# Blocks of the turned node pairs copied from the X tile on the chip instead of loaded from DRAM, in a one-core graph layer

## The chip, the cores and the metric

The kernel runs on one core of a Trainium2 chip. The metric is the device time of one execution in microseconds (us), as the median over runs. The profile is of one further execution, whose span (first to last instruction) and device time are given below.

## What is computed

A graph layer over N = 50000 nodes with 512 features, in float32. Cut to what matters:

```python
msg  = x[src]                                    # 62500 edges, one of them a loop at every node
agg  = segment_sum(msg, dst, n);  deg = segment_sum(ones, dst, n)
mean = agg / maximum(deg, 1)[:, None]
h    = mean @ W_l + b + x @ W_r
out  = layernorm(x + h * sigmoid(h))             # over the 512 features
```

Only 12500 edges are not loops. The kernel therefore computes `x @ (W_l + W_r) + b` for all nodes, and a correction row for each of the few nodes that have other edges.

## The kernel before, in words

There are five in-order queues: SP (SyncE, which issues nearly all plain transfers), POOL (gathers by index and the small rstd work), PE (TensorE), ACT (ScalarE) and DVE (VectorE). An instruction waits on semaphores at the head of its queue, and all that stands behind it on that queue waits too. Every queue's order is written out by hand, step by step over t.

The nodes lie in 391 tiles of 128 rows. Three stages follow each other. In the **early stage** (to about 180 us) the products of the first 44 tiles are made and put into DRAM, while DVE works out index lists. In the **edge stage** (to about 503 us) 98 tiles of edges give the correction rows. In the **node stage** the remaining 347 tiles are worked off as NP = 174 pairs of tiles, and one of the 44 "light" tiles is finished in every fourth pair. The change touches the node stage and the last steps of the edge stage on SP.

A pair t goes through these steps, with the function and line of each:

- SP loads its 256 rows into slot t mod 4 of the tile `X` (`load_x`, L321). It first waits until `residual` of pair t-4 is done (`u_made`, L319), as that was the last reader of the slot.
- PE needs the pair with features on the partitions. For an even pair PE turns it itself: 8 transposes of `X` into PSUM (`transpose_x`, L634). An odd pair is turned "by blocks" (`by_blocks`, L206; 86 pairs, t = 1, 3, ..., 171): SP loads the rows once more from DRAM into `x_raw`, with blocks of 32 rows placed so that DVE's transpose of 32 x 32 blocks (`turn_blocks`, L1093, from `x_raw` into `x_blocks`) gives a usable order. For these pairs PE uses weights with permuted rows (`wb_hi`, `wb_lo`).
- ACT rounds the turned pair into `x_hi` (`round_x`, L791 for blocks, L795 otherwise), DVE makes the rest `x_lo` (`split_x`, L1081 and L1084).
- PE multiplies: 24 matmuls of 128x512 a pair (`three`, L530) onto a PSUM bank that ACT has seeded with the gathered correction rows (`seed`, L817).
- ACT applies silu (L829), DVE adds `X` (`residual`, L1110, which releases the slot of `X`), DVE takes moments (L1118, L1121), POOL makes rstd, DVE `shift` (L1128), ACT normalises into `O` (L805), SP stores `O` (`store_out`, L339).

What sets the order around the change:

- SP's step t (`move`, L374) is: load the blocks of pair t+3 if t+3 is odd; `load_x(t+3)`; `store_out(t-3)`; a store or two loads for the light tile. There is one buffer `x_raw`. `load_blocks(p)` waits until pair p-2 has been turned (L327) and then issues four transfers of 128 KB each.
- DVE's step t (`node_pair`, L1168) is: moments(t-2), split_x(t+1), residual(t-1), shift(t-2), one light operation, and, for odd t, `turn_blocks(t+2)`. So the turn of pair t+2 stands on DVE right behind residual(t-1) and ahead of moments(t-1), split_x(t+2) and residual(t).
- ACT's step t (L849) is: silu(t-1), round_x(t+1), seed(t+1), resetting of the `cor` slot of pair t+3, light work, normalise(t-3).
- In the edge stage SP loads the blocks of pair 1 in step ET-3 (L368 to L371), ahead of the last stores of correction rows (`store_c`, L314); POOL's first gathers in the node stage wait until all of these have landed (L466).

Of the kernel before, what the change touches and what calls it, by code (L numbers as in the profile page):

```python
# [6 lines left out]
def gnn_layer(nc, x, src, dst, w_l, w_r, bias, out):  # L7
# [3 lines left out]
    P = nc.NUM_PARTITIONS  # L11
# [18 lines left out]
    BASE = EARLY * P  # L30
# [13 lines left out]
    with ctx:  # L44
        def sb(name, shape, dt):
            return ctx.enter_context(nc.sbuf_tensor(name, shape, dt))

        def sem(name):
            return ctx.enter_context(nc.semaphore(name))
# [13 lines left out]
        X = sb("X", [P, 4, 2, D], f32)  # L63
# [21 lines left out]
        x_raw, x_blocks = xs[:, 0:2], xs[:, 2:4]  # L85
# [89 lines left out]
        x_in = [sem(f"x_in{b}") for b in range(4)]  # L175
        cor_in = [sem(f"cor_in{b}") for b in range(4)]
        blocks_in, blocks_turned = sem("blocks_in"), sem("blocks_turned")
# [28 lines left out]
        def by_blocks(t):  # L206
            return t % 2 == 1 and t < NP - 1
# [7 lines left out]
        def fixed(v):  # L215
            return isinstance(v, int)

        def wait(eng, s, v):

            if not fixed(v) or v > 0:  # L220
                eng.wait_ge(s, v)

        def peeled(first, end, step):
            for t in range(first, end):
                step(t, t // 4, t % 4)
# [11 lines left out]
        def shifted(t, q, u, by, n, step):  # L237

            if not fixed(t) or 0 <= t + by < n:
                step(t + by, q + (u + by) // 4, (u + by) % 4)  # L240

        def single(t, step):
            step(t, t // 4, t % 4)

        def ring(q, u, n):

            return u % n, q * (4 // n) + u // n
# [7 lines left out]
        def _(sp):  # L255
# [55 lines left out]
            def store_c(t, q, u):  # L311
                b = u % 2
                wait(sp, c_made, t + 1)
                sp.dma_start(corr[bass.ts(t, P), :], c_out[:, b]).then_inc(c_stored[b], 16)  # L314
# [8 lines left out]
                else:  # L323
                    sp.dma_start(X[0:rows, b, 0], x[BASE + t * 2 * P:N, :]).then_inc(x_in[b], 16)

            def load_blocks(t):
                wait(sp, blocks_turned, (t + 1) // 2 - 1)  # L327
                first = BASE + 2 * t * P
                for j in range(4):
                    sp.dma_start(x_raw[32 * j:32 * j + 32].rearrange("r a (i c) -> r (a i) c", i=4),  # L330
                                 x[first:first + 2 * P, j * P:(j + 1) * P].rearrange("(i r) c -> r i c", r=32)
                                 ).then_inc(blocks_in, 16)

            def store_out(t, q, u):
                nt, rows = pair_shape(t)
# [8 lines left out]
            def load_light(l):  # L344
                wait(sp, light_u, l)
                sp.dma_start(l_x[:], x[bass.ts(l, P), :]).then_inc(light_in, 16)
                sp.dma_start(l_h[:], early_product[bass.ts(l, P), :]).then_inc(light_in, 16)
# [5 lines left out]
            def light(q, u):  # L353
                if u == 2:
                    light_at(q - 1, store_light)
                if u == 3:
                    light_at(q + 1, load_light)
# [4 lines left out]
            def edge_tile(t, q, u):  # L362

                shifted(t, q, u, 4, ET, load_row)
                store_c(t, q, u)
                if fixed(t) and ET - 6 <= t < ET - 3:
                    single(t - (ET - 6), load_x)
                if fixed(t) and t == ET - 3:  # L368
                    load_light(0)
                    sp.wait_ge(diff_made, ET)  # L370
                    load_blocks(1)  # L371
            peeled(0, ET, edge_tile)

            def move(t, q, u):  # L374
                if by_blocks(t + 3):
                    load_blocks(t + 3)
                shifted(t, q, u, 3, NP, load_x)
                shifted(t, q, u, -3, NP, store_out)
                light(q, u)
            peeled(0, NP, move)  # L380
            light_tail(light, NP, 4 * EARLY)
            for t in range(NP - 3, NP):
# [484 lines left out]
        def _(dve):  # L867
# [219 lines left out]
                                    ALU.subtract).then_inc(lo_made, 1)  # L1087

            def turn_blocks(t, q, u):
                dve.wait_ge(blocks_in, 64 * ((t + 1) // 2))  # L1090
                if t > 1:
                    dve.wait_ge(lo_made, t - 1)
                v.transpose(x_blocks, x_raw).then_inc(blocks_turned, 1)  # L1093
# [60 lines left out]
            def light(q, u):  # L1154
                if u == 0:
                    light_at(q - 1, light_make_shift)
                if u == 1:
                    light_at(q, light_add)
                if u == 2:
                    light_at(q, light_residual)  # L1160
                if u == 3:
                    light_at(q, light_moments)

            single(0, split_x)
            single(ET - 1, finish)
            single(1, turn_blocks)

            def node_pair(t, q, u):  # L1168
                if t == 1 or t == 2:
                    single(t - 1, add_cor)  # L1170
                shifted(t, q, u, -2, NP, moments)
                shifted(t, q, u, 1, NP, split_x)
                shifted(t, q, u, -1, NP, residual)
                shifted(t, q, u, -2, NP, make_shift)
                light(q, u)
                if by_blocks(t + 2):
                    single(t + 2, turn_blocks)
            peeled(0, NP, node_pair)
            single(NP - 2, moments)
            single(NP - 1, residual)  # L1180
# [27 lines left out]
```

## Time and profile before

| | us |
|---|---|
| median of 3 runs | 1562.06 (1561.3 to 1563.25) |
| profiled execution, device time | 1561.28 |
| profiled execution, span | 1559.5 |
| PE busy | 1517.1 (97%) |
| DVE busy | 1322.9 (85%) |
| ACT busy | 1184.5 (76%) |
| POOL busy | 1008.4 (65%) |

Device time and span differ by 1.8 us. The share of busy time is an average over the three stages. The profile's page gives it, its chain of work tells which engine's work ended last, and the timeline and the sums by window tell the same for the node stage alone. Rows marked SPq are transfers being issued by SP's queue: the time of such a row is the time that the issue holds the queue, not the transfer's own.

### The profile page before, as it was taken

Reading aid. Unit: us, or ns where it says so; the run is one execution under the profiler, and the core shown is the slowest. Engines: PE = TensorE matmul, PEld = TensorE weight load, DVE = VectorE, ACT = ScalarE, POOL = GpSimd, SP = SyncE. Lnnn points to the kernel's source line nnn. Section 1 sums busy time; section 2 is a strip of 40 time slices with the busy share of each in tenths; the row PEclk is TensorE's granted clock in tenths of the full one; section 3 lists DMA queues with packets and bytes.
Section 4 is the critical chain, followed back from the end, with each engine's and each line's share of the span. In section 5 each row is a group of like instructions: output and inputs, shape, how many; then the busy total and the mean of one; then the engine's idle time right before and its main releaser. Section 6 shows DMA issues by size and latency. Waiting matters only on the chain.

```text
span 1559.5 us, 23957 instructions
## 1 busy us (share of the span) xinstructions
PE 1517.1 (97%) x7198; PEld 1244.9 (80%) x7198; DVE 1322.9 (85%) x2088; ACT 1184.5 (76%) x1609; POOL 1008.4 (65%) x1097
## 2 busy tenths in 40 slices
PE   7799999999999899999999999999999999999996
PEld 6688778888887788888888888888888888888884
DVE  7699999999998788888878888888888888888886
ACT  4354333333334799999989999999999999999996
POOL 6466556666662767766757767767667676676673
PEclk9999999999999999999999999999999999999998
DMA  5655588888887689999999999899999999999995
GB/s 191 172 178 188 170 243 266 263 257 271 262 266 231 185 263 286 273 274 278 269 267 286 275 278 271 275 274 277 270 288 268 283 272 276 274 277 267 283 267 182
DMA packets 298965, 397.68 MB, mean 255 GB/s; under 512 B 42652, under 2 KB 144822, under 8 KB 298837
## 3 DMA queue, kind: packets, MB, share of 16 engines
q1 hardware_dynamic: 250855, 321.43, 68.8%
q0 software_dynamic: 46944, 74.22, 17.5%
q8 instruction: 58, 0.95, 0.3%
q14 instruction: 70, 0.57, 0.1%
q10 hardware_dynamic: 1038, 0.50, 0.1%
HBM read 335.97 MB, written 139.67 MB: 305 GB/s over the span
## 4 chain that ended last, share of the span: by engine, by line
PE 90%; DVE 3%; ACT 2%; DMA 2%; issue 2%; SPq 0%; POOL 0%; POOLq 0%; DVEq 0%; ACTq 0%
PE pH L530 81%; PE pT L634 5%; PE pT L603 3%; PE pT L541 1%; DMA cor<-correction_rows,node_idx 1%; ACT O L805 1%; DMA light_x<-in_x 1%; DVE Z L905 1%; ACT cor L751 0%; DVE cor L896 0%; DMA wr_raw<-in_L_gnn_W_r 0%; DVE w_sum L900 0%; DVE Z L900 0%; ACT pH L817 0%; DVE w_sum L905 0%
## 5 line engine op out<-in xcount | busy, mean ns | idle before, releaser
L442 POOL DMA_INDIRECT cor<-correction_rows,node_idx x347 | 395.6, 1140 | 259.2 <-ACT cor L751 186.0
L530 PE MATMUL pH<-ws_hi,x_hi 128*128 128x512 f32 x876 | 348.7, 398 | 6.6 <-ACT pH L817 4.2
L530 PE MATMUL pH<-ws_hi,x_lo 128*128 128x512 f32 x876 | 343.9, 393 | 0.0
L530 PE MATMUL pH<-ws_lo,x_hi 128*128 128x512 f32 x876 | 343.6, 392 | 0.0
L530 PE MATMUL pH<-wb_hi,x_hi 128*128 128x512 f32 x688 | 280.1, 407 | 0.0
L530 PE MATMUL pH<-wb_hi,x_lo 128*128 128x512 f32 x688 | 273.1, 397 | 0.0
L530 PE MATMUL pH<-wb_lo,x_hi 128*128 128x512 f32 x688 | 272.9, 397 | 0.0
L805 ACT ACTIVATE O<-Z,shift,rstd 128x512 f32<-128x512 f32 x347 | 262.4, 806 | 3.6 <-DVE shift L1128 3.6
L1118 DVE BATCH_NORM_STATS2 stats<-Z 128x6 f32<-128x512 f32 x347 | 219.4, 673 | 0.3 <-issue 0.3
L1110 DVE TENSOR_TENSOR Z<-Z,X 128x1024 f32<-128x1024 f32 x174 | 211.3, 1215 | 2.9 <-ACT Z L829 2.9
L829 ACT ACTIVATE Z<-pH 128x1024 f32<-128x1024 f32 (+1 forms) x172 | 175.2, 1019 | 48.5 <-PE pH L530 48.2
L726 ACT ACTIVATE s_hi<-sums 128x512 fp32r<-128x512 f32 x98 | 62.0, 633 | 196.4 <-DVE sums L1029 196.4
L530 PEld LDWEIGHTS pH<-ws_hi,x_hi 128*128 128x128 f32 x876 | 165.8, 189 | 43.9 <-issue 9.0
L530 PEld LDWEIGHTS pH<-ws_hi,x_lo 128*128 128x128 f32 x876 | 165.6, 189 | 35.2
L530 PEld LDWEIGHTS pH<-ws_lo,x_hi 128*128 128x128 f32 x876 | 166.4, 190 | 33.7
L1084 DVE TENSOR_TENSOR x_lo<-pT,x_hi 128x1024 fp32r<-128x1024 f32 x88 | 107.0, 1216 | 95.0 <-ACT x_hi L795 95.0
L751 ACT ACTIVATE cor<-bias_rows 128x1024 f32<-128x1024 f32 x174 | 182.9, 1052 | 0.0
L817 ACT ACTIVATE pH<-cor 128x1024 f32<-128x1024 f32 (+1 forms) x172 | 175.4, 1020 | 7.2 <-DMA cor<-correction_rows,node_idx 7.1
L498 POOL TENSOR_TENSOR rstd<-var_eps,minus_half 128x2 f32<-128x2 f32 x174 | 166.4, 956 | 14.5
L530 PE MATMUL pH<-wl_hi,s_hi 128*128 128x512 f32 x392 | 163.3, 417 | 2.6 <-DVE s_lo L1036 1.3
L442 POOL DMA_INDIRECT xd<-in_x,dst_idx x98 | 99.3, 1013 | 92.4 <-DVE diff L1019 89.9
L530 PE MATMUL pH<-wl_hi,s_lo 128*128 128x512 f32 x392 | 157.3, 401 | 0.0
(148 smaller groups left out, 2767.9 us busy)
## 6 DMA issues: line engine op xcount, KB each, us to landing
X<-in_x SPq DMA_DIRECT2D x173, 512.0 KB, 4.5
out<-O SPq DMA_DIRECT2D x173, 512.0 KB, 4.8
xs<-in_x SPq DMA_DIRECT2D x344, 128.0 KB
correction_rows<-c_out SPq DMA_DIRECT2D x98, 256.0 KB, 4.1
light_x<-in_x SPq DMA_DIRECT2D x58, 256.0 KB, 2.8
light_h<-early_product SPq DMA_DIRECT2D x44, 256.0 KB
out<-light_o SPq DMA_DIRECT2D x44, 256.0 KB, 4.1
join_row<-joined SPq DMA_DIRECT2D x98, 64.0 KB, 4.0
```

The lines of the kernel that those rows point to most:

```text
L442: g.indirect_dma_start(out=out_, out_offset=None, in_=table, in_offset=bass.IndirectOffsetOnAxis(ap=idx, axis=0), bounds_check=bound, oob_ ...
L498: g.tensor_tensor(rstd[0:rows, b, 0:nt], var_eps[0:rows, b, 0:nt], minus_half[0:rows, 0:nt], ALU.pow).then_inc(rstd_made, 1)
L530: last = mm(ps, a[:, k], w[:, k], start=(n == 0 and not onto), stop=(n == len(terms) - 1), skip_group_check=onto)
L634: last = nc.tensor.transpose(pT[u % 2][:, a, k * P:k * P + rows], X[0:rows, b, a, k * P:(k + 1) * P], eye[0:rows, 0:rows])
L726: a_(s_hi[b][:], sums[:, b, :, 2:], ACT.Copy).then_inc(s_hi_made, 1)
L751: a_(cor[u][:], bias_rows[:].rearrange("p (a n) -> p a n", a=1).to_broadcast([P, 2, D]), ACT.Copy).then_inc(cor_reset, 1)
L805: last = a_(O[0:rows, b, a], Z[0:rows, u % 4, a], ACT.Identity, scale=rstd[0:rows, b, a:a + 1], bias=shift[0:rows, b, a:a + 1])
L817: a_(pH[u % 2][0:rows, 0:nt], cor[b][0:rows, 0:nt], ACT.Copy).then_inc(seeded, 1)
L829: a_(Z[0:rows, b, 0:nt], h, ACT.Silu).then_inc(silu_made, 1)
L1084: v.tensor_tensor(x_lo[b][:, :, 0:nt, 0:rows].rearrange("p k a r -> p a k r"), pT[b][:, 0:nt].rearrange("p a (k r) -> p a k r", k=K)[:, :, ...
L1110: v.tensor_tensor(Z[0:rows, b, 0:nt], Z[0:rows, b, 0:nt], X[0:rows, b, 0:nt], ALU.add).then_inc(u_made, 1)
L1118: v.bn_stats(stats[0:rows, u % 2, a], Z[0:rows, u % 4, a]).then_inc(stats_made, 1)
```

## The change

SP no longer loads the blocks from DRAM. It waits until the pair's rows have landed in `X` (`x_in`) and the buffer `x_raw` is free, and copies the blocks from `X` to `x_raw` with sixteen transfers of 32 KB. This is issued in SP's step t for pair t+2, behind `load_x(t+3)`, where it was step t for pair t+3, ahead of `load_x(t+3)`. DVE's turn waits for all sixteen. In DVE's program the turn moves from the end of step t (pair t+2) to the start of step t+1 (again pair t+2). `single(1, turn_blocks)` ahead of the loop becomes the first instruction of step 0.

```diff
-            def load_blocks(t):
+            def copy_blocks(t):
+                b, used = ring(t // 4, t % 4, 4)
+                sp.wait_ge(x_in[b], 16 * (used + 1))
                 wait(sp, blocks_turned, (t + 1) // 2 - 1)
-                first = BASE + 2 * t * P
-                for j in range(4):
-                    sp.dma_start(x_raw[32 * j:32 * j + 32].rearrange("r a (i c) -> r (a i) c", i=4),
-                                 x[first:first + 2 * P, j * P:(j + 1) * P].rearrange("(i r) c -> r i c", r=32)
-                                 ).then_inc(blocks_in, 16)
+                for i in range(4):
+                    for j in range(4):
+                        sp.dma_start(x_raw[32 * j:32 * j + 32, :, i * P:(i + 1) * P],
+                                     X[32 * i:32 * i + 32, b, :, j * P:(j + 1) * P]).then_inc(blocks_in, 16)
@@ edge_tile on SP
                     sp.wait_ge(diff_made, ET)
-                    load_blocks(1)
+                    copy_blocks(1)
@@ move
-                if by_blocks(t + 3):
-                    load_blocks(t + 3)
                 shifted(t, q, u, 3, NP, load_x)
+                if by_blocks(t + 2):
+                    copy_blocks(t + 2)
                 shifted(t, q, u, -3, NP, store_out)
@@ turn_blocks
-                dve.wait_ge(blocks_in, 64 * ((t + 1) // 2))
+                dve.wait_ge(blocks_in, 256 * ((t + 1) // 2))
@@ node_pair on DVE
-            single(1, turn_blocks)
             def node_pair(t, q, u):
+                if by_blocks(t + 1):
+                    single(t + 1, turn_blocks)
                 ...
                 light(q, u)
-                if by_blocks(t + 2):
-                    single(t + 2, turn_blocks)
```

## Rows read from the trace of the kernel before

**Rows 1.** The page: busy time by engine, then the chain that ended last.

```profile
PE 1517.1 (97%) x7198; PEld 1244.9 (80%) x7198; DVE 1322.9 (85%) x2088; ACT 1184.5 (76%) x1609; POOL 1008.4 (65%) x1097
...
PE 90%; DVE 3%; ACT 2%; DMA 2%; issue 2%; SPq 0%; POOL 0%; POOLq 0%; DVEq 0%; ACTq 0%
```

**Rows 2.** Sums by window (columns: window, its length, busy time by engine, clock, DMA share).

```profile
521.30:1522.50 1001.20, 1001.09 (x4692) 826.40 (x4692) 836.25 (x1469) 949.25 (x1130) 696.85 (x798) 1.00 0.94 274
```

**Rows 3.** One line's instructions, DVE's turn: duration min/median/max in ns, first and last start.

```profile
L1093 DVE STREAM_TRANSPOSE xs<-xs x86: 1225/1237/1247, 502.5 to 1522.5; 128x1024 f32<-128x1024 f32 x86
```

**Rows 4.** Timeline of DVE in the node stage (start, duration, instruction, idle before).

```profile
899.38 1.22 DVE L1110 TENSOR_TENSOR Z<-Z,X 128x1024 f32<-128x1024 f32 x1
...
901.18 1.24 DVE L1093 STREAM_TRANSPOSE xs<-xs 128x1024 f32<-128x1024 f32 x1
...
914.08 1.23 DVE L1093 STREAM_TRANSPOSE xs<-xs 128x1024 f32<-128x1024 f32 x1
...
916.70 1.22 DVE L1081 TENSOR_TENSOR x_lo<-xs,x_hi 128x1024 fp32r<-128x1024 f32 x1
917.84 1.22 DVE L1110 TENSOR_TENSOR Z<-Z,X 128x1024 f32<-128x1024 f32 x1
...
922.13 1.22 DVE L1084 TENSOR_TENSOR x_lo<-pT,x_hi 128x1024 fp32r<-128x1024 f32 x1 [0.71 <-ACT x_hi L795]
923.27 1.22 DVE L1110 TENSOR_TENSOR Z<-Z,X 128x1024 f32<-128x1024 f32 x1
```

**Rows 5.** Timeline of SP's queue in the same stretch.

```profile
900.62 0.37 SPq L321 DMA_DIRECT2D X<-in_x  x1
...
902.67 2.71 SPq L330 DMA_DIRECT2D xs<-in_x  x4
```

**Rows 6.** Timeline of ACT in the same stretch.

```profile
915.61 1.05 ACT L791 ACTIVATE x_hi<-xs 128x1024 fp32r<-128x1024 f32 x1
...
921.07 1.03 ACT L795 ACTIVATE x_hi<-pT 128x1024 fp32r<-128x1024 f32 x1
```

**Rows 7.** One line's instructions: issue times of three kinds of transfer on SP.

```profile
L264 SPq DMA_DIRECT2D early_product<-light_o x22: 319/326/430, 21.8 to 176.4; - x22
...
L339 SPq DMA_DIRECT2D out<-O x173: 372/400/795, 530.5 to 1550.1; - x173
...
L330 SPq DMA_DIRECT2D xs<-in_x x344: 327/497/1548, 497.1 to 1515.9; - x172
```

**Rows 8.** Transfers by line: count, KB of each, median us from issue to landing.

```profile
X<-in_x SPq DMA_DIRECT2D x173, 512.0 KB, 4.5
...
join_row<-joined SPq DMA_DIRECT2D x98, 64.0 KB, 4.0
...
early_product<-light_o SPq DMA_DIRECT2D x22, 256.0 KB, 2.0
...
X<-in_x SPq DMA_DIRECT2D x1, 160.0 KB, 2.2
```

**Rows 9.** Timeline of SP's queue where the node stage begins.

```profile
497.05 1.91 SPq L330 DMA_DIRECT2D xs<-in_x  x4
499.00 3.92 SPq L314 DMA_DIRECT2D correction_rows<-c_out  x2
...
519.04 1.81 SPq L330 DMA_DIRECT2D xs<-in_x  x4
```

**Rows 10.** Timeline of DVE there.

```profile
516.05 1.22 DVE L1110 TENSOR_TENSOR Z<-Z,X 128x1024 f32<-128x1024 f32 x1
...
517.78 1.24 DVE L1093 STREAM_TRANSPOSE xs<-xs 128x1024 f32<-128x1024 f32 x1
```

**Rows 11.** Timeline of PE there.

```profile
517.90 0.77 PE L530 MATMUL pH<-ws_hi,x_hi 128*128 128x512 f32 x1 [4.16 <-ACT pH L817]
```

**Rows 12.** Sums by window (columns as in rows 2).

```profile
517.88:521.30 3.42, 3.39 (x8) 2.75 (x9) 3.42 (x4) 2.00 (x3) 1.75 (x3) 0.50 0.68 216
...
1548.70:1559.50 10.80, 0.00 (x0) 0.00 (x0) 1.78 (x5) 3.55 (x5) 1.47 (x4) 0.50 0.30 107
```

## Prediction, written before the changed kernel was built or run

> **What bounds the kernel now.** I read the page first: PE is busy 97% of the span, and the chain of work that ended last is 90% PE [rows 1]. Then the sums by window, for the node stage alone: from 521.3 to 1522.5 us PE is busy 1001.09 of 1001.20 us, at full clock, while DVE is busy 836 and ACT 949 [rows 2]. So here PE never waits, and no work taken from another engine can shorten the stage. What can lengthen it is a wait that PE's inputs cannot make up for.
>
> One round of the node stage is two pairs, an odd one turned by blocks and an even one. DVE's turn stands once in a round: 86 turns [rows 3], pair 3's at 517.78 [rows 10], pair 171's at 1522.5, which is 84 rounds later. (1522.5 - 517.8) / 84 = 11.96 us a round.
>
> Then the timelines of DVE and SP side by side, which decide this case. Residual(t-1) runs from 899.38 to 900.60 [rows 4]. SP's load of X for pair t+3 starts at 900.62 [rows 5], since it waits for that residual to free the slot. DVE's turn of pair t+2 starts at 901.18 [rows 4], 0.58 us after the residual. The four block loads that SP issues at 902.67, as soon as that turn has freed `x_raw`, are those of the next odd pair, t+4 [rows 5]. They hold SP until 905.38 and are used by the turn at 914.08: 8.7 us for landing.
>
> **The change part by part.**
>
> *DVE's order.* The turn of pair t+2 leaves the end of step t and stands at the start of step t+1. Nothing stands between these two places, so DVE runs the same instructions in the same order, pair 1's turn too. This costs nothing. Only the count that it waits for is new.
>
> *Bytes.* Each odd pair still moves 512 KB through the same transfer engines, from X instead of DRAM. PE does not wait for transfers in rows 2, so less DRAM reading gains nothing.
>
> *SP's order* is where the time goes. The copies of pair t+2 are issued in SP's step t behind `load_x(t+3)`, and that waits for residual(t-1), the instruction just ahead of this pair's turn on DVE. Before, blocks were issued a whole round ahead of their turn; now residual, X load, sixteen issues, landing and turn follow one another. Behind the waiting turn DVE holds moments(t-1), split_x(t+2), residual(t) and, further on, residual(t+1), for which SP's next copies wait. This is a closed loop through DVE and SP. No buffer and no head start of an engine softens it: a round cannot be shorter than the loop's length. I add it up.
>
> 1. From the turn's start to the end of residual(t+1). In the round from 914.08 the second residual after the turn is the row at 923.27, which ends at 924.49: 10.41 us [rows 4]. Most of it stays when PE has time: the turn ends at 915.31, x_hi of the block pair starts at 915.61 [rows 6], x_lo and a residual follow at 916.70 and 917.84, and the second x_lo at 922.13 starts when ACT has made its x_hi, 921.07 + 1.03 [rows 4, 6]. ACT reaches that only after seed, reset, normalise and silu. Of the 10.41 about 0.45 is ACT waiting for PE, which falls away (9.95); rounds whose ACT step has two light operations are about 1 us longer (10.9). I take 10.4.
> 2. The X load ahead of the copies: 0.02 until it starts, 0.37 for its issue [rows 5], 0.05 to the next: 0.44.
> 3. Sixteen issues. No transfer from X to `x_raw` is in the trace. Four block loads in a quiet stretch took 1.81 us, 0.45 each with the gap [rows 9]; in the busy stretch they took 2.71, 0.68 each [rows 5]. A store from SBUF has a minimum of 0.319 [rows 7], and `out` stores have a median of 0.40 [rows 7]. I take 0.45, as the transfer engines have more room in a longer round: 7.2 us. Bounds 5.1 (16 x 0.319) and 10.8 (16 x 0.68). The size of a transfer hardly shows in these issue times, so cutting 128 KB into 32 KB gives nothing back.
> 4. Landing of the last copy after its issue ends. A 160 KB load at the quiet end landed 2.2 us after its issue began, 256 KB stores in 2.0, `join_row` (64 KB, busy stage) in 4.0 [rows 8]. Less the issue itself this is 1.7 to 3.6. I take 1.9, as each copy is small and the fifteen before it land while it is issued.
>
> Sum of the loop: 10.4 + 0.44 + 7.2 + 1.9 = **19.9 us a round** against 11.96. With all bounds at their low ends it is 9.95 + 0.44 + 5.1 + 1.7 = 17.2, with all at the high ends 10.9 + 0.44 + 10.8 + 3.6 = 25.7. Even the lowest is far over 11.96.
>
> The Trainium skill speaks against the change here: "DMA: Bandwidth & Descriptors", Rules for kernel authors, says to join many small transfers, as those under 64 KB pay mostly overhead. Its fit for transfers of the gpsimd path (section Anatomy of one DMA) gives an estimate of 2.1 us for 32 KB, where the rows have 2.0 to 2.2 for larger ones; with it as item 4 the round would be 20.1 us.
>
> *The new wait for X.* Pair t+2's X load is issued after residual(t-2), the first residual of a round. That residual ends 5.0 us after the turn (917.84 + 1.22 - 914.08) [rows 4], and the copies begin some 10.8 us after it. That leaves 5.8 us against 4.5 for landing [rows 8]: hidden.
>
> *What is queued behind the copies on SP*: store_out(t-3) and the light tile's transfers, up to 7 us later than now. The `O` slot is needed again a round later, so this hides in a 20 us round.
>
> *Start of the node stage.* Pair 1's blocks are issued ahead of the last two stores of correction rows. Four issues from 497.05 took 1.91 [rows 9], sixteen take 7.2, to 504.2. The last store was issued near 502.6 (499.00 + 3.92 - 0.32) [rows 9] and now goes out near 504.5, and all gathers of the node stage wait for it: +1.9 us.
>
> *End.* After pair 171's turn the span had 37.0 us (1559.5 - 1522.5). Now PE has no work left over at that point. Turn to x_lo 3.8 (916.70 + 1.22 - 914.08) [rows 4], 2.5 pairs at half of 11.96 are 14.9, slower matmuls after a PE idle about 1.7, then the 10.8 us behind PE's last matmul [rows 12]: 31.2.
>
> *Total.* Residual(0) ended at 517.27 [rows 10] and moves to 519.2. Pair 3's turn: 519.2 + 0.44 + 7.2 + 1.9 = 528.7. Pair 171's: + 84 x 19.94 = 2203.7. End: + 31.2 = 2234.9 us of span, + 1.8 = **2237 us** of device time. The median before is 0.8 us above the profiled execution, which I leave out.
>
> **The rivals.**
>
> *PE's clock falls and PE becomes the bound.* PE works 12 us of a 20 us round and idles near 8 in one piece. In the trace a PE idle of 4.16 us [rows 11] stands right before a stretch at half clock (0.50, that is 1.2 of 2.4 GHz), in which 8 matmuls took 3.42 us, 0.43 each [rows 12]. A whole round at that level needs 48 x 0.43 + 8 transposes of about 0.2 = 22.2 us, over the loop's 19.9: 2237 + 84 x 2.3 = 2430 us. Against it: in rows 12 the clock was back after 3.4 us, and such a stretch in each round costs PE 1.7 us, inside its idle time. "TensorE: Matmul & The Clock Gate", The HAM clock gate, in the Trainium skill says that an idle array is gated to half its clock and activity releases it; by this rule rounds begin at half clock, and the trace agrees. Chance 0.05.
>
> *The queue is clogged.* Every issue takes the 0.68 of the busy stretch and landing 3.6: 10.4 + 0.44 + 10.8 + 3.6 = 25.2, giving 2237 + 84 x 5.3 = 2682 us. For it: L330's longest issue is 1.548 [rows 7]. Against it: the bytes of a round spread over a longer round. Chance 0.09.
>
> *Issues far cheaper than any row*, say 0.1 each: 10.4 + 0.44 + 1.6 + 1.7 = 14.1, giving 1750 us. Nothing in rows 7 speaks for it. Chance 0.02.
>
> *Hidden, not slower.* Copies read from an X that is already there, so if they were issued early enough the turn would never wait, PE would stay the bound, and the time would be 1562 us. This decides in favour of no change once items 3 and 4 together are under 11.96 - 9.95 - 0.44 = 1.6 us a round. Landing alone takes 1.7 [rows 8]. Chance 0.02.
>
> **How the numbers follow.** The forecast has 0.80, and 0.02 is left for a gain that I do not see. Issue time alone at its ends gives 2237 - 84 x 2.1 = 2061 and 2237 + 84 x 3.6 = 2539 us; landing alone 2220 and 2380; all low ends together 2237 - 84 x 2.7 = 2010. The range 2010 to 2600 takes in all of these and the clock's rival, and leaves out the clogged queue and the two quick cases. A change of 0.2%, 3 us, is about what a measurement of this kernel can tell from none. Slower 0.96, same 0.02, faster 0.02.
>
> **What would show it right or wrong.** Right: turns near 20 us apart; SP rows of sixteen issues behind each X load, about 7 us long; DVE's turn with 8 to 9 us of idle before it, released by the copies; PE busy near 70% of the span, with pieces at half clock; the second x_lo still released by ACT. Wrong: turns near 12 us apart with no idle time before them; or turns over 22 us apart with PE busy without a break at half clock; or the idle time before the turn ended by X loads rather than by the copies.

## The result and the profile after

The changed kernel takes 2479.16 us (median of 4 runs, 2477.19 to 2480.03) against 1561.68 for the kernel before: 1.5857 times as long, with a 95% interval of 1.5831 to 1.5882. The forecast was 2237, with a range of 2010 to 2600. The profiled execution has a span of 2478.2 us. Where a run below has no interval, its time is that of one execution.

The page of the changed kernel, first busy time by engine, then the chain that ended last, by engine:

```profile
PE 1712.8 (69%) x7198; PEld 1377.8 (56%) x7198; DVE 1328.8 (54%) x2088; ACT 1184.4 (48%) x1609; POOL 1111.7 (45%) x1097
...
SPq 34%; ACT 20%; PE 17%; DVE 11%; issue 11%; DMA 7%; ACTq 0%; POOL 0%; POOLq 0%; DVEq 0%
```

The chain line of [rows 1] had 90% PE. Now SP's queue, issuing transfers, has a third of the chain, and PE has 17%. PE's share of busy time is down to 69%.

The one-line views of DVE's turn and of the copies on SP (duration min/median/max in ns, first and last start), and the waits that matter (us in total, times, longest):

```profile
L1094 DVE STREAM_TRANSPOSE xs<-xs x86: 1245/1245/1246, 509.1 to 2442.2; 128x1024 f32<-128x1024 f32 x86
...
L332 SPq DMA_DIRECT2D xs<-X x1376: 585/597/1769, 497.4 to 2440.3; - x197
...
DVE xs L1094 <- DMA xs<-X: 939.3, 86, 12.5
...
PE pH L531 <- DVE x_lo L1082: 717.5, 85, 10.3
...
SPq L321 <- DVE Z L1111: 729.6, 169, 14.1
```

The last of these lines is SP's X load waiting for `residual`. Pair 3's turn is at 536.2 and pair 171's at 2442.2, so a round takes (2442.2 - 536.2) / 84 = 22.69 us, where [rows 3] gave 11.96. DVE now waits for the copies ahead of each of its 86 turns, 10.9 us on average, and PE waits for the x_lo that follows the turn. In [rows 4] the turn had no idle time noted before it.

One round on the timelines of SP and DVE, which answer to [rows 4] and [rows 5], with pair 3's turn ahead of it:

```profile
1221.26 0.38 SPq L321 DMA_DIRECT2D X<-in_x  x1
...
1227.27 0.38 SPq L321 DMA_DIRECT2D X<-in_x  x1
1227.74 10.93 SPq L332 DMA_DIRECT2D xs<-X  x16
1238.71 0.59 SPq L340 DMA_DIRECT2D out<-O  x1
```

```profile
536.22 1.25 DVE L1094 STREAM_TRANSPOSE xs<-xs 128x1024 f32<-128x1024 f32 x1 [12.12 <-DMA xs<-X]
...
1216.30 1.25 DVE L1094 STREAM_TRANSPOSE xs<-xs 128x1024 f32<-128x1024 f32 x1 [11.27 <-DMA xs<-X]
...
1226.02 1.22 DVE L1111 TENSOR_TENSOR Z<-Z,X 128x1024 f32<-128x1024 f32 x1
...
1239.98 1.25 DVE L1094 STREAM_TRANSPOSE xs<-xs 128x1024 f32<-128x1024 f32 x1 [10.84 <-DMA xs<-X]
...
1247.53 1.23 DVE L1085 TENSOR_TENSOR x_lo<-pT,x_hi 128x1024 fp32r<-128x1024 f32 x1 [0.26 <-ACT x_hi L796]
1248.67 1.21 DVE L1111 TENSOR_TENSOR Z<-Z,X 128x1024 f32<-128x1024 f32 x1
```

The whole loop can be read here. From the turn at 1216.30 to the residual's end at 1227.24: 10.94. To the first copy at 1227.74, with the X load between: 0.50. Sixteen issues to 1238.67: 10.93. Landing until the turn at 1239.98: 1.31. The four make 23.68 us. They follow one another, so that they add up to the round is no finding; that each hand-over is short is one. SP issues its X load 0.03 us after the residual, the copies follow at once, and the turn's idle time is ended by the copies. The next turn-to-residual stretch, a round without the two light operations on ACT, takes 9.90.

### The profile page after: what moved, and what is told of

Same layout as the page of the kernel before. It is cut to its first block, busy times and chain, and to the rows that moved or that the text cites. A ratio compares the mean times of both kernels' runs of the same rounds, so it can differ in the third digit from the quotient of the medians.

```text
span 2478.2 us, 25075 instructions
## 1 busy us (share of the span) xinstructions
PE 1712.8 (69%) x7198; PEld 1377.8 (56%) x7198; DVE 1328.8 (54%) x2088; ACT 1184.4 (48%) x1609; POOL 1111.7 (45%) x1097
## 4 chain that ended last, share of the span: by engine, by line
SPq 34%; ACT 20%; PE 17%; DVE 11%; issue 11%; DMA 7%; ACTq 0%; POOL 0%; POOLq 0%; DVEq 0%
SPq L332 32%; PE pH L531 14%; DMA xs<-X 6%; ACT O L806 5%; DVE Z L1111 4%; DVE xs L1094 4%; ACT pH L818 3%; ACT cor L752 3%; ACT x_hi L796 3%; ACT Z L830 3%; PE pT L604 2%; SPq L321 1%; ACT light_z L834 1%; ACT light_cor L757 1%; PE pT L542 1%
## 5 line engine op out<-in xcount | busy, mean ns | idle before, releaser
L531 PE MATMUL pH<-wb_hi,x_hi 128*128 128x512 f32 x688 | 359.1, 522 | 721.8 <-DVE x_lo L1082 717.5
L531 PEld LDWEIGHTS pH<-wb_hi,x_hi 128*128 128x128 f32 x688 | 176.2, 256 | 781.6 <-issue 739.9
L1094 DVE STREAM_TRANSPOSE xs<-xs 128x1024 f32<-128x1024 f32 x86 | 107.1, 1245 | 939.3 <-DMA xs<-X 939.3
L496 POOL TENSOR_SCALAR var_eps<-mv 128x2 f32<-128x2 f32 x174 | 147.2, 846 | 969.2 <-DVE mv L1122 966.4
L792 ACT ACTIVATE x_hi<-xs 128x1024 fp32r<-128x1024 f32 x86 | 90.9, 1057 | 938.2 <-DVE xs L1094 938.2
L531 PE MATMUL pH<-wb_lo,x_hi 128*128 128x512 f32 x688 | 339.7, 494 | 0.0
L531 PE MATMUL pH<-wb_hi,x_lo 128*128 128x512 f32 x688 | 333.4, 485 | 0.0
L499 POOL TENSOR_TENSOR rstd<-var_eps,minus_half 128x2 f32<-128x2 f32 x174 | 194.5, 1118 | 14.5
L531 PEld LDWEIGHTS pH<-wb_lo,x_hi 128*128 128x128 f32 x688 | 176.8, 257 | 40.3
L531 PEld LDWEIGHTS pH<-wb_hi,x_lo 128*128 128x128 f32 x688 | 171.6, 249 | 47.3
```

What stands on the lines that cost most here:

```text
L496: g.tensor_scalar(var_eps[0:rows, b, 0:nt], mv[0:rows, b, 0:nt, 1], EPS, None, ALU.add).then_inc(eps_added, 1)
L499: g.tensor_tensor(rstd[0:rows, b, 0:nt], var_eps[0:rows, b, 0:nt], minus_half[0:rows, 0:nt], ALU.pow).then_inc(rstd_made, 1)
L531: last = mm(ps, a[:, k], w[:, k], start=(n == 0 and not onto), stop=(n == len(terms) - 1), skip_group_check=onto)
L792: a_(in_blocks(x_hi[b]), x_blocks.rearrange("p a (i k r) -> p (a i) k r", k=K, r=32), ACT.Copy).then_inc(hi_made, 1)
```

## The experiments

All are edits of the changed kernel, and the text after each diff is what stood on record before it ran. The diffs are cut to the lines that matter. For each I read the same four terms from the timelines, as means over the rounds. "Work" is the turn to the residual ahead of the X load, "X" from there to the first of the issues, "issues" from the first one's start to the last one's end, "landing" from there to the next turn. The late kernels are those in which the blocks are issued behind the X load.

| kernel | issue, median | work | X | issues | landing | sum | round | us |
|---|---|---|---|---|---|---|---|---|
| changed kernel | 0.597 | 10.44 | 0.51 | 10.45 | 1.30 | 22.70 | 22.69 | 2479 |
| 16 from DRAM, late | 0.427 | 10.44 | 0.50 | 7.82 | 1.35 | 20.11 | 20.11 | 2256 |
| 4 from DRAM, late | 0.451 | 10.44 | 0.50 | 2.08 | 5.01 | 18.03 | 18.03 | 2077 |
| 4 copies, late | 0.597 | 10.45 | 0.51 | 2.69 | 2.32 | 15.97 | 15.96 | 1899 |
| 16 half copies, late | 0.591 | 10.44 | 0.51 | 10.27 | 1.21 | 22.43 | 22.43 | 2457 |
| 4 copies of 128 rows, late | 0.627 | 10.44 | 0.51 | 2.78 | 3.11 | 16.84 | 16.85 | 1974 |

The four terms cover the round from turn to turn without a gap, so the sum must be the round; it shows nothing by itself. What the table shows is that work and X are the same in all six, to 0.01 us, while the rounds go from 15.96 to 22.69: only the issues and the landing move the time.

**Sixteen from DRAM in the late place.**

```diff
-                                     X[32 * i:32 * i + 32, b, :, j * P:(j + 1) * P]).then_inc(blocks_in, 16)
+                                     x[first:first + 2 * P, j * P:(j + 1) * P]
+                                     .rearrange("(a p) c -> p a c", p=P)[32 * i:32 * i + 32]).then_inc(blocks_in, 16)
```

> The changed kernel with one edit: the sixteen 32 KB transfers read the same blocks from DRAM instead of from X; place and waits stay. Theory (a loop of about 10.4 us of DVE and ACT work + 0.5 X load + sixteen issues + landing, and an issue takes 0.60 us + 0.04 gap because both ends lie on the chip): the issue falls to about 0.41 + 0.04, sixteen take 7.2, landing 2.2, so a round 20.3 us instead of 22.7 and about 2480 - 84 x 2.4 = 2280 us. Rival (the issue takes 0.60 because many small transfers follow one another on one queue, whatever they read): issue unchanged, landing about 2.2, 2480 to 2560 us. Rival (PE's half clock makes the round): no round under 22 us, 2430 to 2480 us.

Measured: 2255.71 us, a round of 20.11.

```profile
L333 SPq DMA_DIRECT2D xs<-in_x x1376: 311/427/2167, 497.2 to 2217.2; - x197
```

The same number, size, shape and place, with only the source changed: the issue fell from 0.597 to 0.427. So the rival of small transfers on one queue is out as the source of the 0.60. The kernel is still 44% slower than before, so the source was not the main cost.

**Four from DRAM in the late place.** The four loads of the kernel before, put behind the X load; the turn waits for 64.

```diff
-                for i in range(4):
-                    for j in range(4):
-                        sp.dma_start(x_raw[32 * j:32 * j + 32, :, i * P:(i + 1) * P],
-                                     X[32 * i:32 * i + 32, b, :, j * P:(j + 1) * P]).then_inc(blocks_in, 16)
+                for j in range(4):
+                    sp.dma_start(x_raw[32 * j:32 * j + 32].rearrange("r a (i c) -> r (a i) c", i=4),
+                                 x[first:first + 2 * P, j * P:(j + 1) * P].rearrange("(i r) c -> r i c", r=32)
+                                 ).then_inc(blocks_in, 16)
```

> The changed kernel with the four 128 KB loads from DRAM of the kernel before, in the changed kernel's place behind the X load, so the place alone. Theory (loop): 10.4 + 0.5 + 4 x 0.45 + 2.5 of landing = 15.2 us a round, 2480 - 84 x 7.5 = 1850 us, well over the 1562 of before. Rival (place costs nothing, number of transfers does): 1562 us. Rival (PE's half clock makes the round): 2430 to 2480 us.

Measured: 2077.25 us, a round of 18.03. The place alone, with the transfers themselves as before, costs 33%. That rules out a place that costs nothing and PE's clock as the cause. My number was 230 us too low, mainly by one term: landing took 5.01 where I had 2.5. In this kernel the block loads have all been issued about 2.5 us after the X load's issue began, and X loads land 4.2 us after theirs at the median of this kernel's transfers; the last block lands later still. Behind sixteen issues X has landed by then. That the X load is what delays the blocks is my reading; no run takes it away.

**Four copies only.**

```diff
-                for i in range(4):
-                    for j in range(4):
-                        sp.dma_start(x_raw[32 * j:32 * j + 32, :, i * P:(i + 1) * P],
-                                     X[32 * i:32 * i + 32, b, :, j * P:(j + 1) * P]).then_inc(blocks_in, 16)
+                for i in range(4):
+                    sp.dma_start(x_raw[32 * i:32 * i + 32, :, i * P:(i + 1) * P],
+                                 X[32 * i:32 * i + 32, b, :, i * P:(i + 1) * P]).then_inc(blocks_in, 16)
```

> The changed kernel with only the four copies whose block stays in its own 32 partitions (i = j); the other twelve blocks of each pair are left out and the turn waits for four. Theory (loop, 0.64 us a copy): 22.7 - 12 x 0.64 = 15.0 us a round, 2480 - 84 x 7.7 = 1835 us. Rival (PE's half clock makes the round): 2430 to 2480 us, as PE's work is unchanged.

Measured: 1898.54 us, a round of 15.96. PE's work is what it was, yet the round fell by 6.7 us: PE's clock does not make it. The twelve issues saved are worth 7.8 us a round, and landing took back 1.0, which I had not counted. That is why the time is above the 1835 expected.

**Sixteen from DRAM in the early place.** Number alone: the sixteen read from DRAM as in the late place, and are issued in step t for pair t+3, ahead of the X load and without the wait for X.

```diff
+                if by_blocks(t + 3):
+                    copy_blocks(t + 3)
                 shifted(t, q, u, 3, NP, load_x)
-                if by_blocks(t + 2):
-                    copy_blocks(t + 2)
```

> Sixteen 32 KB loads from DRAM in the place of the kernel before (a round ahead, in front of the X load, no wait for X), so the number alone. If an issue is 0.45 us with its gap as theory has it for DRAM: 7.2 us of issues, the blocks are there 3 us ahead of their turn, 1562 to 1580 us. If an issue stays at 0.64 for small transfers (rival): issues 10.2 us, SP holds 13 us of work in a round of 12, and x_raw's own loop (turn 1.2 + 10.2 + landing 2.5 = 13.9 us) gives 1562 + 84 x 2 = 1730 us.

Measured: 1671.35 us, 1.0705 times the kernel before (95% interval 1.0677 to 1.0734), a round of 13.26. Between my two numbers. A median issue is 0.428, but a sixteen takes 8.93 on average, and SP's queue has hardly any room left. Its timeline:

```profile
999.73 8.62 SPq L331 DMA_DIRECT2D xs<-in_x  x16
1008.39 0.43 SPq L321 DMA_DIRECT2D X<-in_x  x1
1008.86 0.58 SPq L340 DMA_DIRECT2D out<-O  x1
1009.48 0.47 SPq L352 DMA_DIRECT2D out<-light_o  x1
1009.99 1.32 SPq L321 DMA_DIRECT2D X<-in_x  x1
1011.35 1.04 SPq L340 DMA_DIRECT2D out<-O  x1
1012.44 0.57 SPq L347 DMA_DIRECT2D light_x<-in_x  x1
1013.05 0.54 SPq L348 DMA_DIRECT2D light_h<-early_product  x1
1013.63 9.45 SPq L331 DMA_DIRECT2D xs<-in_x  x16
```

Each row begins where the one before ends: 13.9 us of issues from one sixteen to the next, more than the 11.96 that PE needs. Every other round lacks the light tile's three transfers and is shorter, which gives the 13.26. What I had left out for the case of cheap issues is that the other issues of the round become longer too: an X load 1.32 and a store 1.04, against 0.37 in [rows 5] and 0.40 in [rows 7]. Why they become longer, no run here shows.

**Half the bytes.** Copies of one of the two tiles.

```diff
-                        sp.dma_start(x_raw[32 * j:32 * j + 32, :, i * P:(i + 1) * P],
-                                     X[32 * i:32 * i + 32, b, :, j * P:(j + 1) * P]).then_inc(blocks_in, 16)
+                        sp.dma_start(x_raw[32 * j:32 * j + 32, 0, i * P:(i + 1) * P],
+                                     X[32 * i:32 * i + 32, b, 0, j * P:(j + 1) * P]).then_inc(blocks_in, 16)
```

> The changed kernel with copies of one of the pair's two tiles: sixteen copies of 16 KB (32 rows of 512 bytes) instead of 32 KB (64 rows); the other tile's blocks are left out. If the 0.60 us of an issue is a price per transfer: issue 0.60, round 22.7, 2480 us. Rival (a price per row or byte): issue down to about 0.45, sixteen take 7.8 us, round 20.2, 2270 us.

Measured: 2456.88 us, issue 0.591 at the median. Half the rows and bytes save 0.006 us an issue: a price per transfer, not per row or byte.

**Four copies of 128 rows that stay in their partitions.**

```diff
-                for i in range(4):
-                    for j in range(4):
-                        sp.dma_start(x_raw[32 * j:32 * j + 32, :, i * P:(i + 1) * P],
-                                     X[32 * i:32 * i + 32, b, :, j * P:(j + 1) * P]).then_inc(blocks_in, 16)
+                for j in range(4):
+                    sp.dma_start(x_raw[:, :, j * P:(j + 1) * P],
+                                 X[:, b, :, j * P:(j + 1) * P]).then_inc(blocks_in, 16)
```

> The changed kernel with four copies of 128 KB from X to x_raw that keep their 128 partitions (no block changes its partitions, so the blocks are not placed as the turn needs them); the turn waits for four. If both ends on the chip make the issue 0.60: issue 0.60 here too, four take 2.5 us, and with the 5 us of landing that four 128 KB loads had behind the X load the round is 10.4 + 0.5 + 2.5 + 5 = 18.4, about 2110 us. Rival (the 32-partition shape makes it): issue about 0.40, round 17.7, 2050 us. The issue time decides, the round only adds up.

Measured: 1974.32 us, below both numbers, as landing took 3.11 where I had 5. The issue time was to decide:

```profile
L331 SPq DMA_DIRECT2D xs<-X x344: 594/627/1532, 497.4 to 1935.2; - x172
```

0.627 an issue with 128 partitions and four times the bytes: neither the 32-partition shape nor the size makes the price. What the 0.59 to 0.63 have in common, against 0.427 and 0.451, is that both ends lie on the chip. One end there is not enough: `out` stores from SBUF to DRAM have 0.40 [rows 7]. Why an issue with both ends on the chip holds the queue longer, no run here shows.

**Two queues.** ACT's queue issues eight of the sixteen ahead of its silu.

```diff
+            def copy_half(t):
+                b, used = ring(t // 4, t % 4, 4)
+                act.wait_ge(x_in[b], 16 * (used + 1))
+                wait(act, blocks_turned, (t + 1) // 2 - 1)
+                for i in range(2, 4):
+                    for j in range(4):
+                        act.dma_start(x_raw[32 * j:32 * j + 32, :, i * P:(i + 1) * P],
+                                      X[32 * i:32 * i + 32, b, :, j * P:(j + 1) * P]).then_inc(blocks_in, 16)
```

> The changed kernel with eight of the sixteen copies issued by ACT's queue ahead of its silu (from pair 3 on), eight by SP. Theory (each queue pays 0.64 us an issue on its own): eight take 5.1 us, round 10.4 + 0.5 + 5.1 + 1.5 = 17.5 to 18.5, 2040 to 2130 us. Rival (one maker of transfers behind both queues sets the pace): issue about 1.2 us on each queue, round 22.7, 2480 us.

Measured: 2143.22 us, a round of 18.73.

```profile
L332 SPq DMA_DIRECT2D xs<-X x696: 585/598/2352, 496.3 to 2103.4; - x174
...
L856 ACTq DMA_DIRECT2D xs<-X x680: 592/619/2226, 522.1 to 2102.4; - x170
```

0.598 on one queue and 0.619 on the other, at the same time: the price is paid by the queue that issues, not by something shared behind both. The round is 0.2 us over the upper end that I gave; landing was 2.27 where I had 1.5, and the cause of that is open. The Trainium skill says in "DMA: Bandwidth & Descriptors", Issuing engines are not separate DMA queues, that issuing from several engines only saves the time it takes to initiate the transfer, usually small beside the transfer itself. The first half agrees with this run: SP's issues fell from 10.45 to 5.53 us a round, and landing rose. The "usually" does not hold here: in the changed kernel sixteen issues took 10.45 us, and the last copy landed 1.30 after them.

**Ahead of the X load.**

```diff
-                shifted(t, q, u, 3, NP, load_x)
                 if by_blocks(t + 2):
                     copy_blocks(t + 2)
+                shifted(t, q, u, 3, NP, load_x)
```

> The changed kernel with the copies of pair t+2 issued ahead of the X load of pair t+3 instead of behind it. The last residual of the round is then out of the loop; what is left is turn to the first residual 5.0 + X load of the pair itself to landing 4.0 + sixteen issues 10.3 + landing 1.3 = 20.7 us, 2478 - 84 x 2.0 = 2310 us. Rival (the sixteen issues are all that counts and their place in the step nothing): 2480 us. Rival (out of the loop, hidden): under 1700 us.

Measured: 2303.26 us, a round of 20.73 (20.7 expected). The copies no longer wait for the residual just ahead of the turn, but for their own X load (85 times, 170.0 us in all), which waits for the first residual of the round. One loop is replaced by another, 2 us shorter.

**Six slots of X, copies a round ahead.** X is loaded five pairs ahead into a ring of six slots, two of them in the edge stage's buffers `xd`.

```diff
-                wait(sp, u_made, t - 3)
+                wait(sp, u_made, t - 5)
...
-                shifted(t, q, u, 3, NP, load_x)
-                if by_blocks(t + 2):
-                    copy_blocks(t + 2)
+                if by_blocks(t + 3):
+                    copy_blocks(t + 3)
+                shifted(t, q, u, 5, NP, load_x)
```

> The copies from X in the place of the kernel before, a round ahead of their turn: the ring of X gets two more slots (in the edge stage's buffers, free by then), X is loaded five pairs ahead, and the sixteen copies of pair t+3 are issued in SP's step t ahead of the X load. Theory: the loop through the residual and the X load is open; what is left is x_raw's own loop on one queue, turn 1.25 + about 0.4 until SP comes to it + 10.25 for sixteen issues + 1.3 of landing = 13.2 us a round against 11.96, so 1562 + 84 x 1.2 = 1665 us. Rival (issued a round ahead the copies hide): 1562 us. Rival (copies inside the chip are slow wherever they stand): over 2000 us.

Measured: 1895.08 us, 1.2134 times the kernel before (95% interval 1.2111 to 1.2157), a round of 15.82. Neither hidden nor over 2000, but 230 us above my number. SP's timeline:

```profile
1000.37 0.59 SPq L325 DMA_DIRECT2D xd<-in_x  x1
...
1002.02 1.50 SPq L344 DMA_DIRECT2D out<-O  x1
1005.03 10.76 SPq L336 DMA_DIRECT2D xs<-xd  x16
1015.84 0.59 SPq L325 DMA_DIRECT2D X<-in_x  x1
1016.47 0.47 SPq L344 DMA_DIRECT2D out<-O  x1
1016.99 0.47 SPq L356 DMA_DIRECT2D out<-light_o  x1
1017.50 1.42 SPq L325 DMA_DIRECT2D X<-in_x  x1
1018.96 0.93 SPq L344 DMA_DIRECT2D out<-O  x1
1019.94 0.55 SPq L351 DMA_DIRECT2D light_x<-in_x  x1
1020.53 0.53 SPq L352 DMA_DIRECT2D light_h<-early_product  x1
1021.16 10.88 SPq L336 DMA_DIRECT2D xs<-X  x16
```

From 1005.03 SP does not rest: 16.1 us of issues from one sixteen to the next. Ahead of it SP rests for 1.5 us. The sixteen at 1005.03 wait for their own pair's X load, issued at 1000.37 right behind the sixteen before, to land. This is so in the rounds without the light tile's three transfers; the waits of SP's queue:

```profile
SPq L336 <- DMA X<-in_x: 40.7, 29, 1.7
...
SPq L336 <- DMA xd<-in_x: 17.7, 13, 1.6
```

With the loop through the residual open, the order of SP's queue is the bound: its own work in one kind of round, and in the other a second loop of sixteen issues, X load and its landing. I had summed `x_raw`'s loop (13.2) and neither of these.

**Six slots and two queues.** As that kernel, with ACT issuing eight copies behind its rounding of the block pair.

```diff
                 shifted(t, q, u, 1, NP, round_x)
+                if by_blocks(t + 3):
+                    copy_half(t + 3)
```

> As the kernel with six slots of X, and eight of the sixteen copies issued by ACT's queue behind its rounding of the block pair. x_raw's loop is now 1.25 + 0.4 + 5.1 + 1.5 = 8.3 us and hides in 11.96. If ACT's queue can issue while its engine computes: 1562 to 1575 us, no gain over the kernel before, since PE sets the time. Rival (the eight issues hold ACT's other work up): ACT has 11 us of work in a round, with 5.1 us of issues 14 to 16 us, 1740 to 1900 us.

Measured: 1925.75 us, 1.2323 times the kernel before (95% interval 1.229 to 1.2356), slightly above the rival's 1900. The turn's wait is gone, and ACT's seeding of the next PSUM bank has taken its place. The two waits of that chain and ACT's timeline:

```profile
ACT pH L824 <- issue: 389.0, 84, 5.2
...
PE pH L537 <- ACT pH L824: 230.1, 85, 6.8
...
999.94 1.06 ACT L798 ACTIVATE x_hi<-xs 128x1024 fp32r<-128x1024 f32 x1 [0.30 <-DVE xs L1110]
1000.02 5.70 ACTq L861 DMA_DIRECT2D xs<-X  x8
1005.83 1.03 ACT L824 ACTIVATE pH<-cor 128x1024 f32<-128x1024 f32 x1 [4.82 <-issue]
```

The eight issues hold ACT's queue for 5.70 us, the seed behind them starts 4.82 us late, and PE waits for the seed: 230 of the 364 us that this kernel is longer than the kernel before. The rest I did not trace to an instruction. No kernel here beats the kernel before; the nearest is 7% behind. With its loads a round ahead the transfers cost PE nothing [rows 2], and there was nothing to gain.

## Why the prediction was right, and where it was off

**The bound and the side of the change.** Right. The node stage was PE's alone [rows 2], and the change made a closed loop: X load, copies, turn, residual. The late kernel with four DRAM loads shows the loop without the copies, at 33%. Work and X stay the same in six kernels, and moving the copies ahead of the X load shortened the round by what the changed loop's sum said (20.73 against 20.7).

**DVE's order costs nothing; less DRAM reading gains nothing.** DVE's busy time is 1328.8 against 1322.9 [rows 1]. On DRAM reading the run with sixteen from DRAM in the late place speaks: with the same blocks read from DRAM again, and all else as in the changed kernel, the time is 223 us lower, not higher.

**Item 1, work of 10.4 us.** Measured 10.44, and 9.90 and 10.94 for the two kinds of round in the rows above, as worked out. The second x_lo is still released by ACT's x_hi.

**Item 2, 0.44.** Measured 0.51.

**Item 3, sixteen issues of 7.2 us.** This is the term that was mis-sized: 10.45. I took 0.45 an issue from the quiet four loads of [rows 9], whose source is DRAM. With a DRAM source a sixteen in this place takes 7.82, near my number; the copies' source is X, and that makes the issue 0.597. No row of before had both ends on the chip. That the bound of 10.8 held it was luck: it came from DRAM loads in a busy stretch, another cause. The reason that I gave for the low value, room in the transfer engines, cannot be ruled out for loads (a sixteen from DRAM took 7.82 in rounds of 20.11 and 8.93 in rounds of 13.26) and does little for copies: their median is 0.59 to 0.62 in every kernel with 32 KB or 16 KB copies. That the size hardly shows was right (0.591 for half).

**Item 4, landing of 1.9 us.** Measured 1.30 behind sixteen issues, so this term was too large and took back a fifth of item 3's error. It is no constant: 2.3 to 5.0 behind four.

**The wait for X** is hidden as forecast: X loads land 4.0 us after their issue, and in the list of SP's waits of the changed kernel the copies do not appear.

**Start and end.** Pair 3's turn came at 536.2 instead of 528.7, since sixteen longer issues also held the last correction rows longer, and pair 3's own sixteen were longer too. The stretch after the last turn took 36.0 us (2478.2 - 2442.2) instead of 31.2, for the most part by a row that I misread. [rows 12] has no matmul after 1548.70, and I took that time for the end of PE's work, 10.8 us before the end. PE's last matmuls, in the kernel before and in the changed one, were these:

```profile
1544.09 0.40 PE L530 MATMUL pH<-ws_hi,x_lo 128*80 128x512 f32 x1
...
2462.82 0.40 PE L531 MATMUL pH<-ws_hi,x_lo 128*80 128x512 f32 x1
```

Both end 15.0 us before the end of the span. Over all, the miss is 7.5 at the start, 84 x (22.69 - 19.94) = 231 in the rounds and 4.8 at the end: 243 us, which is the 2478.2 - 2234.9 of the spans.

**The rival of PE's clock** gave 2430, nearer to the measured time than the forecast, and by the wrong mechanism. Its premise came true. This is PE's timeline in the round above, and behind it the sums of the window from that round's turn on (columns as in [rows 2]):

```profile
1232.72 1.03 PE L635 MATMUL pT<-eye,X 128*128 128x128 f32 x8
1243.88 0.77 PE L531 MATMUL pH<-wb_hi,x_hi 128*128 128x512 f32 x1 [10.13 <-DVE x_lo L1082]
1244.45 0.63 PE L531 MATMUL pH<-wb_lo,x_hi 128*128 128x512 f32 x1
...
1247.54 0.40 PE L531 MATMUL pH<-wb_hi,x_hi 128*128 128x512 f32 x1
...
1239.98:1262.00 22.02, 13.65 (x56) 11.00 (x56) 9.81 (x18) 11.10 (x13) 8.11 (x8) 0.81 0.52 157
```

After 10.13 us without work PE starts with 0.63 us matmuls and is back at 0.40 within 4 us; the granted clock of the window is 0.81 on average, between the two levels of [rows 12] and [rows 2]. But PE works 13.65 of the 22.02 us and waits for x_lo in 85 rounds, so it is not the bound, and the kernel with four copies has the same PE work in rounds of 15.96. A time near a rival's number is no evidence for the rival; the terms are.

**The clogged queue** gave 2682 with issues of 0.68 and landing of 3.6. The issues came near it, by both ends on the chip and not by a full queue; the landing did not. Neither the cheap issues nor the hidden case appeared.

## What to carry to other kernels

Before a transfer is moved on an in-order queue, list what it now stands behind and who waits for it; if the instruction it waits for stands on the same engine just ahead of its reader, the transfer's issue and landing are added to every round, and no idle time elsewhere pays for it. Count a queue's issues as work: sixteen small ones were 8 to 11 us here, the others on a full queue became longer too, and on an engine's own queue they delayed its compute. Look for every loop that closes through the queue: opening one left the next. Take the price of an issue from a transfer with the same two ends, and where the trace has none, keep the far end of the range.

## What was not expected of the hardware

A plain transfer with both ends on the chip held the issuing queue for 0.59 to 0.63 us at the median, where one from DRAM into the same tile held it for 0.43 to 0.50 (the upper value in the kernel before, [rows 7]). It hardly changed with the size (0.591 at 16 KB, 0.597 at 32, 0.627 at 128), with the partitions (32 or 128), or with the queue (0.598 on SP, 0.619 on ACT). Two queues paid it side by side. And the landing of the last block was no constant: with an X load of 512 KB ahead, 1.2 to 1.4 us behind sixteen issues and 2.3 to 5.0 behind four.
